# Four chained models on one core: norm rows on ScalarE, statistics carried over, set-up and last norm of the transformer rearranged

## The reference

```
x = x + layernorm(conv_attention_mixture(layernorm(x)))
x = x + layernorm(fp4_experts(layernorm(x)))
x = x + layernorm(linear_attention(layernorm(x)))
x = x + layernorm(windowed_transformer(layernorm(x)))
```

```
for i in range(6):
    x = attn_layer(shift_tokens(x), ...) + x
    x = ffn_layer(shift_tokens(x), ...) + x
```

## Time and profile before

| | us |
|---|---|
| median of 3 runs (lowest, highest) | 5442.13 (5440.97, 5442.73) |
| the profiled execution | 5434.87 |
| its span, first to last instruction | 5433.2 |
| start of the transformer's set-up block | 1354.06 |
| start of its main block (SyncE's first shift) | 1405.87 |
| end of the last MLP's last sum | 5368.4 |
| start of the last block | 5395.31 |
| one attention tile in a full stretch | 17.2 |

### The profile page before, as it was taken

One profiled execution on the slowest core, in us unless ns is written; L12 is line 12 of the kernel. 1 busy time (PEld: TensorE's weight loads), 2 busy tenths in 40 slices (PEclk: granted clock), 3 DMA queues, 4 the chain that ended last, 5 costly groups with the idle time before them and its releaser, 6 DMA issues. The chain is left out here.

```text
span 5433.2 us, 144088 instructions
## 1 busy us (share of the span) xinstructions
PE 4847.8 (89%) x42260; PEld 4060.2 (75%) x42260; DVE 4003.2 (74%) x11109; ACT 3810.0 (70%) x12437; POOL 2451.6 (45%) x3763
## 2 busy tenths in 40 slices
PE   5988949994299998999989998899989999799994
PEld 3657949984188876888778887788867888688883
DVE  5664757777588876888768887788867888688875
ACT  1334423431199986999869997799968999599982
POOL 0000000000466663666546664566636666366661
PEclk7997959997699998999999999999999999999997
DMA  0001100000111111111111111111111111111111
GB/s 21 2 17 39 39 1 0 0 0 4 49 27 27 27 49 27 27 27 27 51 28 27 27 27 47 29 27 27 27 50 28 27 27 27 51 24 27 27 49 31
DMA packets 103390, 149.33 MB, mean 27 GB/s; under 512 B 65245, under 2 KB 72690, under 8 KB 102386
## 3 DMA queue, kind: packets, MB, share of 16 engines
q1 hardware_dynamic: 93410, 107.27, 8.7%
q0 software_dynamic: 9232, 33.12, 1.9%
HBM read 49.13 MB, written 2.10 MB: 9 GB/s over the span
## 5 line engine op out<-in xcount | busy, mean ns | idle before, releaser
L2023 ACT ACTIVATE d_probs<-d_S_ps,d_neg_max 128x96 f32<-128x96 f32 x3072 | 1000.6, 342 | 13.5 <-DVE d_neg_max L2237 3.8
L1626 POOL TENSOR_TENSOR d_qk<-d_qk,d_sin_terms 128x512 f32<-128x512 f32 x768 | 960.8, 1272 | 29.7 <-DVE d_sin_terms L2209 29.7
L1801 PEld LDWEIGHTS d_S_ps<-d_kT,d_q_blocks 128*128 128x128 f32 x6144 | 791.8, 193 | 2.3
L1801 PE MATMUL d_S_ps<-d_kT,d_q_blocks 128*128 128x96 f32 x6144 | 791.1, 272 | 0.0
L2209 DVE TENSOR_TENSOR d_qk<-d_A_ps,d_tables 128x512 f32<-128x512 f32 x768 | 527.6, 687 | 229.0 <-ACT d_squares L1979 162.6
L2023 ACT ACTIVATION_READ_ACCUMULATOR d_probs<-d_S_ps,d_neg_max 128x1 f32 x3072 | 639.3, 208 | 0.0
L1758 PE MATMUL d_A_ps<-d_wqkv_hi,d_xT_hi 128*128 128x512 f32 x1152 | 556.2, 483 | 22.1 <-DVE d_sin_terms L2209 17.4
L1979 ACT ACTIVATE d_squares<-d_A_ps 128x512 f32<-128x512 f32 x768 | 462.6, 602 | 123.9 <-PE d_A_ps L1760 123.5
L2209 DVE TENSOR_TENSOR d_sin_terms<-d_A_ps,d_tables 128x512 f32<-128x512 f32 x768 | 522.8, 681 | 0.0
L1765 PE MATMUL d_T_ps<-d_ident,d_qk 128*128 128x128 f32 x3072 | 483.9, 281 | 36.5 <-POOL d_qk L1663 32.8
L2031 ACT ACTIVATE d_probsT<-d_PT_ps 96x512 f32<-96x512 f32 (+1 forms) x768 | 459.9, 599 | 79.8 <-PE d_PT_ps L1811 79.6
(11 more groups left out here) (406 smaller groups left out, 10766.6 us busy)
## 6 DMA issues: line engine op xcount, KB each, us to landing
d_v_early<-d_v SPq DMA_DIRECT2D x192, 256.0 KB, 3.0
d_v_early<-d_v SPq DMA_DIRECT2D x192, 128.0 KB, 2.3
d_tables<-L_ffn_rotary POOLq DMA_DIRECT2D x7, 2048.0 KB, 8.3
d_qk<-L_ffn_Wqkv POOLq DMA_DIRECT2D x21, 512.0 KB, 3.9
d_xs<-d_xb SPq DMA_DIRECT2D x56, 127.0 KB
d_xs<-d_xb SPq DMA_DIRECT2D x96, 63.5 KB
ax_fp_blocks<-L_ffn_blocks_gu SPq DMA_DIRECT2D x16, 256.0 KB, 3.7
ax_fp_scales<-L_ffn_scales_gu SPq DMA_DIRECT2D x64, 64.0 KB, 3.0
```

The costliest lines, as they stand in the source:

```text
L1626: nc.gpsimd.tensor_tensor(c4[:, :, s, :], c4[:, :, s, :], s4[:, :, 1 - s, :], ALU.add).then_inc(rotated, 1)
L1801: last = nc.tensor.matmul(S[g % 2][:, n * SEEN:(n + 1) * SEEN], qx[:, p, half, :], kT[b][jj][:, p, HALF * half:HALF * half + SEEN], start= ...
L2023: nc.scalar.activation(pr[:, g, n, seen_columns(g)], S[g % 2][:, n * SEEN:(n + 1) * SEEN], ACT.Exp, bias=nmax[:, g, n:n + 1], accum_out=de ...
```

## The change

1. **Statistics are carried over.** A tile `x_stats` (128 x 32 x 6) lives as long as x. add_normalised writes into it the statistics of the x that it has just summed; normalise_rows (bn, cn) and the transformer's set-up take them (`taken=`) instead of counting. In linear_attention VectorE counts the statistics of y group by group beside ScalarE's copies, and add_normalised (ca) takes those.
2. **add_normalised shares its rows.** ScalarE scales (Identity with scale and bias from memory), VectorE sums in eight groups of 128x512 and counts in between.
3. **Set-up of the transformer.** SyncE issues Wqkv in three parts into three buffers, tables, scales, mask, identity, decay, and then the first two shifts, each as soon as its four tiles of `xb` are scaled. GpSimd only issues Wo and clears. ScalarE does the high parts of Wqkv, 32 scalings for `xs`, 16 for `xb`, and the casts of mask and identity. VectorE does 16 scalings for `xb`, the low parts of Wqkv, the table products, and smaller clearings. The main block's shift loop starts at group 2.
4. **GpSimd's loop** has five turns with `prepare_attention` for the next layer, and a sixth copy of the layer without it behind the loop.
5. **The last norm** moves into the main block: VectorE starts it behind its last residual, in two halves of 16 tiles with a root each; ScalarE scales 48 half-tiles, VectorE 16; sums and stores go by quarters of both sequences. SyncE's stores stand behind its last shift and before its final waits.

```diff
-def add_normalised(nc, ctx, tag, x, y):
+def add_normalised(nc, ctx, tag, x, y, x_stats, taken=None):
...
+            nc.vector.scalar_tensor_tensor(shift[:], mv[:, :, 0], -1.0, rstd[:], ALU.mult, ALU.mult).then_inc(shift_ready, 1)
+            for g in range(GROUPS):
+                sl = slice(G4 * g, G4 * g + G4)
+                v.wait_ge(scaled, G4 * (g + 1))
+                nc.vector.tensor_tensor(x[:, sl, :], x[:, sl, :], y[:, sl, :], ALU.add).then_inc(summed, 1)
+                if g:
+                    v.wait_ge(summed, g)
+                    for n in range(G4 * g - G4, G4 * g):
+                        nc.vector.bn_stats(x_stats[:, n, :], x[:, n, :]).then_inc(next_stat, 1)
+            v.wait_ge(summed, GROUPS)
+            for n in range(N_TILES - G4, N_TILES):
+                nc.vector.bn_stats(x_stats[:, n, :], x[:, n, :]).then_inc(next_stat, 1)
+
+        @block.scalar
+        def _(act):
+            act.wait_ge(shift_ready, 1)
             for n in range(N_TILES):
-                nc.vector.tensor_scalar(y[:, n, :], y[:, n, :], mv[:, n, 0:1], rstd[:, n:n + 1], ALU.subtract, ALU.mult
-                                        ).then_inc(scaled, 1)
-            for g in range(GROUPS):
-                if g % 2:
-                    continue
-                v.wait_ge(scaled, G4 * (g + 2))
-                sl = slice(G4 * g, G4 * (g + 2))
-                nc.vector.tensor_tensor(x[:, sl, :], x[:, sl, :], y[:, sl, :], ALU.add).then_inc(summed, 1)
+                nc.scalar.activation(y[:, n, :], y[:, n, :], ACT.Identity, scale=rstd[:, n:n + 1], bias=shift[:, n:n + 1]
+                                     ).then_inc(scaled, 1)
...
+            @block.vector
+            def _(v):
+                for g in range(GROUPS):
+                    v.wait_ge(y_out, g + 1)
+                    for n in range(G4 * g, G4 * g + G4):
+                        nc.vector.bn_stats(y_stats[:, n, :], y[:, n, :]).then_inc(y_stat, 1)
...
             @block.sync
             def _(sp):
+                for c in range(3):
+                    sp.dma_start(stage[c], w["Wqkv"][0:1, :, c * 1024:(c + 1) * 1024].rearrange("l p n -> p (l n)")
+                                 ).then_inc(weight_in[c], DMA)
+                sp.dma_start(tabs[:, :, 0:J * HD], w["rotary"].rearrange("p a j d -> p a (j d)")).then_inc(tables_in, DMA)
...
+                for g in range(2):
+                    sp.wait_ge(vector_rows, G4 * (g + 1))
+                    if g:
+                        sp.wait_ge(shift_main, DMA * g)
+                        sp.wait_ge(shift_row, DMA * g)
+                    sp.dma_start(xs[1:P, g * 2:g * 2 + 2, :, D // 2:D], xb[0:P - 1, g * 2:g * 2 + 2, :, :]).then_inc(shift_main, DMA)
+                    sp.dma_start(xs[0:1, g * 2 + 1:g * 2 + 3, :, D // 2:D], xb[P - 1:P, g * 2:g * 2 + 2, :, :]
+                                 ).then_inc(shift_row, DMA)
...
+            @block.scalar
+            def _(act):
+                for c in range(3):
+                    act.wait_ge(weight_in[c], DMA)
+                    nc.scalar.activation(wh[:, c * 1024:(c + 1) * 1024], stage[c], ACT.Copy).then_inc(w_hi, 1)
+                act.wait_ge(scaling, 1)
+                for n in range(N_TILES):
+                    nc.scalar.activation(xs[:, n // B, n % B, 0:64], x_outer[:, n, 0:64], ACT.Identity, scale=rstd[:, n:n + 1],
+                                         bias=shift0[:, n:n + 1]).then_inc(scalar_rows, 1)
+                for n in range(BY_VECTOR, N_TILES):
+                    nc.scalar.activation(xb[:, n // B, n % B, :], x_outer[:, n, 64:D], ACT.Identity, scale=rstd[:, n:n + 1],
+                                         bias=shift0[:, n:n + 1]).then_inc(scalar_rows, 1)
...
-                for g in range(GROUPS):
-                    if g:
-                        sp.wait_ge(shift_main, DMA * g)
-                        sp.wait_ge(shift_row, DMA * g)
+                for g in range(2, GROUPS):
+                    sp.wait_ge(shift_main, DMA * g)
+                    sp.wait_ge(shift_row, DMA * g)
...
+                xo = x_outer[:].rearrange("p (j b) d -> p j b d", b=B)
+                for q in range(4):
+                    js = slice(q * J // 4, (q + 1) * J // 4)
+                    for b in range(B):
+                        sp.wait_ge(summed, 4 * q + 2 * b + 2)
+                        sp.dma_start(out[b].rearrange("(j p) d -> p j d", p=P)[:, js, :], xo[:, js, b, :]).then_inc(stored, DMA)
+                sp.wait_ge(stored, 8 * DMA)
                 sp.wait_ge(shift_main, DMA * (GROUPS + DEPTH * SHIFTS))
...
-                with pool.Fori(0, DEPTH) as l:
+                def layer(l):
...
+                with pool.Fori(0, DEPTH - 1) as l:
+                    layer(l)
+                    next_weights(l)
+                layer(DEPTH - 1)
...
+                for half in range(2):
+                    act.wait_ge(end_scaling, half + 1)
+                    for n in range(half * HALF_TILES, (half + 1) * HALF_TILES):
+                        for rows, src in ((end_lo, xs[:, n // B, n % B, 0:64]), (end_hi, xb[:, n // B, n % B, :])):
+                            if half == 0 or rows is end_lo:
+                                nc.scalar.activation(rows[:, n // B, n % B, :], src, ACT.Identity, scale=end_rstd[:, n:n + 1],
+                                                     bias=end_shift[:, n:n + 1]).then_inc(end_rows, 1)
...
+                for half in range(2):
...
+                    for n in tiles:
+                        nc.vector.bn_stats(end_stats[:, n, 0, :], xs[:, n // B, n % B, 0:64]).then_inc(end_stat, 1)
+                        nc.vector.bn_stats(end_stats[:, n, 1, :], xb[:, n // B, n % B, :]).then_inc(end_stat, 1)
...
+                v.wait_ge(end_rows, 2 * HALF_TILES)
+                add_out(0)
+                add_out(1)
+                for n in range(HALF_TILES, N_TILES):
+                    nc.vector.tensor_scalar(end_hi[:, n // B, n % B, :], xb[:, n // B, n % B, :], end_mv[:, n, 0:1], end_rstd[:, n:n + 1],
+                                            ALU.subtract, ALU.mult).then_inc(end_vector_rows, 1)
+                v.wait_ge(end_rows, 3 * HALF_TILES)
+                v.wait_ge(end_vector_rows, HALF_TILES)
+                add_out(2)
+                add_out(3)
```

More of the change, by code:

```diff
@@ L92, in rsqrt_steps, with normalise_rows @@
         rsqrt_step(nc, vec, i, x, y, t, magic, steps, done, waits_met)
-def normalise_rows(nc, ctx, tag, x, xn, xT, ident, even_first=False, scale=None, bias=None):
+def normalise_rows(nc, ctx, tag, x, xn, xT, ident, even_first=False, scale=None, bias=None, taken=None):
     m = Memory(nc, ctx, tag)
-    stats = m.sb("stats", [P, N_TILES, 6])
+    stats = m.sb("stats", [P, N_TILES, 6]) if taken is None else taken
     mv = m.sb("mv", [P, N_TILES, 2])
@@ L163, in add_normalised @@
     rstd = m.sb("rstd", [P, N_TILES])
+    shift = m.sb("shift", [P, N_TILES])
     tmp = m.sb("tmp", [P, N_TILES])
     magic = m.sb("magic", [P, N_TILES], I32)
-    magic_set, stat, steps, waits_met, scaled, summed = (
-        m.sem(s) for s in ("magic_set", "stat", "steps", "waits_met", "scaled", "summed"))
+    magic_set, stat, steps, waits_met, shift_ready, scaled, summed, next_stat = (
+        m.sem(s) for s in ("magic_set", "stat", "steps", "waits_met", "shift_ready", "scaled", "summed", "next_stat"))
     with nc.Block() as block:
@@ new lines, in _ @@
+                v.wait_ge(stat, N_TILES)
+                nc.vector.tensor_scalar(ve[:], mv[:, :, 1], LN_EPS, None, ALU.add).then_inc(stat, 1)
+                v.wait_ge(stat, N_TILES + 1)
+                v.wait_ge(zeroed, 2)
+                rsqrt_steps(nc, v, ve[:], rstd[:], tmp[:], magic[:], steps, 0, waits_met)
+                v.wait_ge(steps, RSQRT_STEPS)
+                nc.vector.scalar_tensor_tensor(shift0[:], mv[:, :, 0], -1.0, rstd[:], ALU.mult, ALU.mult).then_inc(scaling, 1)
+                for n in range(BY_VECTOR):
+                    nc.vector.tensor_scalar(xb[:, n // B, n % B, :], x_outer[:, n, 64:D], mv[:, n, 0:1], rstd[:, n:n + 1],
+                                            ALU.subtract, ALU.mult).then_inc(vector_rows, 1)
@@ L1524, in _ @@
-                for n in range(N_TILES):
-                    for half, dst in ((0, xs[:, n // B, n % B, 0:64]), (1, xb[:, n // B, n % B, :])):
-                        nc.vector.tensor_scalar(dst, x_outer[:, n, 64 * half:64 * half + 64], mv[:, n, 0:1],
-                                                rstd[:, n:n + 1], ALU.subtract, ALU.mult).then_inc(x_ln, 1)
-                v.wait_ge(loaded, 3 * DMA)
-                nc.vector.tensor_copy(mask[:], maskf).then_inc(mbf, 1)
-                nc.vector.tensor_copy(identb[:], ident[:]).then_inc(mbf, 1)
```

204 lines of the change are left out of this document (100 added, 104 removed).

## The result

The changed kernel takes 5365.9 us (median of 4 runs, 5357.8 to 5370.15) against 5441.55 (5440.43 to 5442.73): ratio 0.9854, 95% interval 0.9842 to 0.9866, against a forecast of 5356.4 with the range 5346 to 5370. The profiled execution takes 5368.19, its span 5366.4.

A forecast was written before the change was run, and what follows sets the result against it. Bound by seams where one engine works alone: norm pairs, set-up, SyncE's shift chain, the end. Gains 10.2 + 42.3 + 2 + 31.2 = 85.7 us off the profiled 5434.9 give 5349.2, by median 5356.4; range 5346 to 5370.

The forecast's parts named there:

- norm blocks, start of set-up: Three add_normalised calls: sharing rows and carrying statistics starts the transformer's set-up 3.75 + 3.75 + 2.7 = 10.2 us sooner.
- set-up and first shifts: Transformer's start: early values come 84.1 us behind set-up's start instead of 126.4, gaining 42.3 us.
- last layer (the wait alone): Last MLP: without GpSimd's seventh-layer work, TensorE's 4.0 us wait shrinks; gain between 0 and 4, taken as 2 us.
- end: Last norm and stores: the end comes at 5402.0 instead of 5433.2, gain 31.2 us, set by SyncE's queue.
- (a): Rival, set-up: big loads ahead in ring order hold the first shift, chain 9 us later, 5365 us; chance 0.10.
- (b): Rival, norm blocks and end: ScalarE's rows don't overlap (0.48 each at 128 columns), 5368 us; chance 0.06.
- first shift at 9: Sign, set-up: the first token shift is issued 9 us behind the block's start, bounds +2 / -1.
- table loads ahead of ScalarE's rows: Sign of being wrong, set-up: table loads appearing before ScalarE's rows would show the prediction wrong.
- Bounds 0 and 2 us; I take 1: Set-up: delay of a VectorE scaling beside a GpSimd clearing, taken as 1 us, between 0 and 2.
- (d): Rival, transformer's start: something else in the first tile holds the early values, no gain there, 5399 us; chance 0.03.
- (c): Rival, last layer: GpSimd's copied layer starves for instructions as code run once, 5455 us; chance 0.02.
- 7.3 us under the median: Whole kernel: the profiled execution's distance below the three runs' median, carried over from 5349.2 to 5356.4.

The follow-up runs named there:

- before_again: The kernel before, unchanged, run once more for its profile: 5434.4 us against 5441.1, ratio 0.9988.
- The repeat: The changed kernel, unchanged, timed again beside other kernels: 5360.62 us, ratio 0.9849 to the kernel before.
- clear_late: Changed kernel, but GpSimd starts its seven clearings only when VectorE has scaled its 16 rows: 5360.56 us, ratio 0.9841 to the kernel before.
- pool_loads: Changed kernel with GpSimd clearing behind VectorE's 16 rows and issuing the large loads instead of SyncE: 5360.83 us, ratio 0.9852 to the kernel before.
- setup_old: Changed kernel with the transformer's old set-up and SyncE's old first shifts: 5396.59 us, ratio 0.9913 to the kernel before.
- early_first: Changed kernel with the first early values in SyncE's queue behind the fourth shift instead of the eighth: 5343.46 us, ratio 0.9819 to the kernel before.
- best_a: Changed kernel with GpSimd's clearings later, two units' early values moved up in the shift chain, no shifts behind the last MLP: 5330.68 us, ratio 0.9789 to before.

## Why the prediction was right, and by how much it was off

The terms read from the traces are these; the start of set-up is compared with before_again, whose clock rose as late as the changed kernel's:

| term | forecast | measured |
|---|---|---|
| norm blocks, start of set-up | 10.2 | 1359.66 - 1349.70 = 10.0 |
| set-up and first shifts | 42.3 | 126.4 - 89.4 = 37.0 |
| last layer (the wait alone) | 2 | 4.0 - 2.8 = 1.2 |
| end | 31.2 | 30.6 |
| sum | 85.7 | 78.8 |

The whole-kernel gains, 75.6 and 82.0, lie around 78.8. The first row sets one execution against one: over the ten profiles with the changed norm blocks and the late clock it would be 8.6 to 11.0.

**What was luck.** The mechanisms were right, but 5365.9 lies just above the 5346 to 5365 that the forecast's own bounds gave. It is inside the stated range only because that was widened for rivals (a) and (b), and neither came about in the changed kernel. Rival (a)'s 5365 is even the nearest number, with a hold that the trace does not have. The repeat's 5360.6 is inside both. Of the signs, first shift at 9 (13.7), third at 28 to 29 (32.7) and early values at 84 (89.4) failed, all by the one stall below; the rest came true. One sign of being wrong, table loads ahead of ScalarE's rows, could tell nothing, since the change itself issues them first (1351.02, the rows from 1362.54).

**Norm blocks.** Right in mechanism and size: ScalarE's pitch is 0.387, VectorE stays inside it, and ScalarE sets the pace. Rival (b), rows that don't overlap, is refuted by 12.42 us for 32.

**Set-up: the mis-sized term.** "Bounds 0 and 2 us; I take 1": a scaling beside GpSimd's clearings cost 7.3 (7.44 - 0.18), outside the bounds. I had looked at the first scaled row, where the clearings are nearly over, and not at the first tensor_scalar of the block, which adds a constant to 32 variances ahead of the root at t0 + 2.5. Every step of the root stands behind it. The stall cost 6.3 us more than priced; 1.5 of them came back, since without it the first shift is issued at t0 + 6.5 (clear_late) and not at t0 + 8. So the first shift came 4.7 us late, outside its bound of +2. That is 4.7 of the 5.3 us missing; the other 0.6 are in the chain's eight steps (67.6 + 8.1 instead of 67.3 + 7.75).

**The loads beside the first shift.** I had added 0.5 us for them. This step looked right (second shift 9.48 behind the first) only because the stall kept shift and loads apart; clear_late shows 15.3 us between the two. Rival (a) named a real hold, 5.8 us in clear_late, but its mechanism, the order of one queue, is not what decides, since pool_loads has the hold from two queues. In the changed kernel it cost nothing. With the first shift where it came, the forecast would have been 5356.4 + 4.7 = 5361.

**The chain covers the rest.** Right: TensorE waits 27.3 us for the early values (forecast some 25), and the products and casts on VectorE and ScalarE cost nothing. Rival (d) is refuted by setup_old and early_first. The prediction took the step of the chain, 9.56 us, as given. A window of the changed kernel inside the second shift (length; busy PE, PEld, DVE, ACT, POOL; clock; DMA share; GB/s) shows what fills it:

```profile
1375.00:1379.00 4.00, 0.00 (x0) 0.00 (x0) 2.03 (x3) 4.00 (x12) 0.00 (x0) 0.50 0.08 17
```

The 16 transfer engines are 0.08 busy, little more than one of them, and move 17 GB/s, where the loads had 418. At that rate the 127 KB of a shift take 7.5 us. No run here changed the transfer's shape.

**Last layer and rival (c).** The 4.0 us wait became 2.8, so 1.2 of the 2 us are shown, within 0 to 4; most of the wait is there without GpSimd's multiplication too. Whether the clock behind it gains more is open. No attention tile is slower in GpSimd's separate copy.

**End.** Right in all steps: 8.4 us to the first half's shift (forecast 8.7, though its printed terms add to 8.5; the sum does not use it), stores behind the last shift. best_a shows that without the useless shifts the first store starts with VectorE's sums.

**The rest of the distance.** The forecast carried the profiled execution's 7.3 us under the median over to the changed kernel, whose medians scatter: 5365.9 and 5360.6. In two profiles of the same changed kernel the early values come at 1439.08 and 1439.33, and the spans are 5366.4 and 5356.6. From the early values to the last residual they take 3893 and 3883 us; the kernel before takes 3888 and 3898 there. The last attention tile of the second layer, between its residual sum and the one before, shows one piece of these ten us, in the changed kernel and then in its repeat (window as above):

```profile
2630.29:2649.13 18.84, 13.92 (x118) 12.02 (x118) 12.92 (x54) 12.54 (x43) 8.96 (x9) 0.67 0.59 198
```

```profile
2628.98:2645.10 16.12, 11.04 (x118) 9.46 (x118) 10.83 (x54) 12.43 (x43) 9.31 (x9) 0.89 0.62 199
```

The same 118 matmuls take 2.7 us longer with a granted clock of 0.67 of full instead of 0.89. Two more pieces, of 1.9 us each, come behind the first layer and at the last attention tile of the fifth. They lie at the seams, where one stage passes into the next. What tips the clock there is open; no run here varied it by itself.

## What to carry to other kernels

Where one engine can lock another out, price the first instruction of the blocked kind behind the start, not the one whose result you want, and, as here, at the whole chain of the other engine's work. When you take one delay away, ask what would have held the same step a few us later: here a 7.3 us stall, taken away, gave back 1.4, because transfers stood right behind it. Where a queue puts urgent work behind work that nobody needs yet, look at its order first: the early values of two units moved up took TensorE's wait from 27.3 to 0.6 us. Look too at what the transfers of a chain move while they last; these moved 17 GB/s. And do not take a difference of a few us in a stretch from one profile of each kernel: the last layer's stretch read 37.4 or 40.8 us with the same code.

## What the runs showed of the hardware

- A 128x32 tensor_scalar on VectorE stood 7.44 us beside GpSimd's seven clearings in a row, 0.18 without them; 31 aggregations of statistics, the last of which ran beside the first clearing, took 2.10 us, as without (2.11).
- The issue of a shift's row part takes 6.5 us by itself, 12.3 behind all loads, 8.4 with 2 MB fewer ahead, and 14.1 with the loads in GpSimd's queue: an issue can stand for the transfers of others.
- A shift of 127 partitions from on-chip memory to on-chip memory moves 17 to 18 GB/s, with the transfer engines 0.08 busy.
- TensorE's first long stretch at full clock began at 106 or at 120 to 123 us in executions of the same code, worth 5.6 us at set-up. At seams the same tile took 16.1 us at a granted clock of 0.89 or 18.8 at 0.67.
